# Layer 1: gate columns of all sixteen tiles first, the shared expert's up products afterwards from turned halves kept on chip

## The chip, the core and the metric

The kernel runs on one core of one Trainium2 chip. The metric is the device time of one execution, in microseconds (us); smaller is better. Engines are named as in the profile: PE (TensorE), PEld (its weight loads), DVE (VectorE), ACT (ScalarE), POOL (GpSimd) and SP (SyncE, which issues DMAs).

## What is computed

The input x has 4 x 512 tokens of 256 channels, here 16 tiles of 128 tokens. A mixture-of-experts block, a recurrent block and the same mixture-of-experts block again are added to it; the two passes through the first block are "layer 0" and "layer 1" below (`f` = 0 and 1).

```python
def ffn(x):                                   # x is layer-normalised
    scores = sigmoid(gate_w @ x) + gate_b     # 16 experts
    weights, indices = top_k(scores, 4); weights /= weights.sum(-1)
    shared = (silu(x @ w1_shared) * (x @ w3_shared)) @ w2_shared
    h3 = silu((x @ w1_routed[e]) * (x @ w3_routed[e]))     # for the 4 chosen e
    return shared + sum(weights * (h3 @ w2_routed[e]))
x = x + 0.5 * ffn(layernorm(x))
x = x + recurrence(layernorm(x))
x = x + 0.5 * ffn(layernorm(x))
```

## The kernel before

Everything is written out by hand: each engine has its own program, run in its order, and engines wait for each other by semaphores. The order of the code is the order of the work.

**The token phase of layer 1.** It runs from the end of the recurrence to the first expert tile. POOL normalises the 16 tiles (`norm`, L571). For each tile PE turns it into channels by tokens (`turn_x`, L1487, two transposes), ACT copies the result out of PSUM in a rounded format (the high half, `xs_high`, L741), and DVE subtracts to get the low half (`xs_low`, L1003). PE then forms the up products of the shared expert and the gate's logits in one accumulation of 2 x 176 + 16 = 368 columns (`hidden`, L1490, through `mm3`, L1414): three terms (high by high, low by high, high by low) for each of two channel halves, six matmuls, each with another 128-column stationary operand. The loop at L1582 turns tile s and then multiplies tile s - 2. ACT copies 16 logits (`logits`, L749) and applies silu to the first 176 columns (`silu`, L745), and DVE multiplies by the other 176, read from PSUM (`product`, L1008). SP writes the result to DRAM (`hid_out`, L471), where the end of the layer fetches it.

**The routing.** ACT applies the sigmoid to the logits of tiles 0 to 12 and of tiles 13 to 15 (`sigmoid`, L755). DVE takes the four best of 16 (`route_members`, L1033 to L1043), PE counts tokens per expert (`count`, L1558 and L1560), DVE works out each row's slot (`route_slots`, L1065 to L1099) and then, for each tile, builds two 0/1 matrices (`pick`, L1108 and L1110), which in layer 1 compare the table `hcst` with numbers in `stage`, both in SBUF. ACT scales one of them (`scale_pick`, L791), and PE multiplies them (L1574) into the list of token numbers, which DVE copies out at the end (L1121). Only then POOL begins to fetch rows by that list (`gather`, L578), and the loop over 79 expert tiles starts.

**The weights split again.** In layer 0 the weights of the routed experts are split into high and low parts. The recurrence overwrites those of experts 12 to 15. In layer 1 SP loads them again (`load_late`, L453 and L454), ACT makes the high parts (`high_expert`, L668 and L671), and POOL the low parts (`low_expert`, L547, 512 and 704 columns for an expert). PE waits for them before the first expert tile (L1606).

Of the kernel before, what the change touches and what calls it, by code (L numbers as in the profile page):

```python
# [7 lines left out]
H = 176  # L8
# [23 lines left out]
LAG_HID = 5  # L32
# [39 lines left out]
MW = 3 * DC * D  # L72
UP_AGAIN = [sum(e >= MAMBA_E for e in u) for u in (DVE_UP, POOL_UP)]
# [13 lines left out]
def build(nc, x_d, w13r_d, w2r_d, w13s_d, w2s_d, wm_d, cst_d, hcst_d, out_d):  # L87
# [7 lines left out]
    with ctx:  # L95
# [20 lines left out]
        mroom = nc.alloc_sbuf_tensor_at("mamba_room", [P, (NE - MAMBA_E) * 2 * WE], f32, offset=w_base + MAMBA_E * 2 * WE * 4)  # L116
        stage = [sb("stage0", [P, WSH]), sb("stage1", [P, WE])]
# [11 lines left out]
        hT = [[ring_r[:, 1024 + (b * 2 + h) * 256:1024 + (b * 2 + h + 1) * 256] for h in range(2)] for b in range(2)]  # L129
        ring_g = sb("ring_g", [P, (XG - UN) * D])  # L130
        xg = [ring_f[:, k * D:(k + 1) * D] for k in range(UN)] + [ring_g[:, k * D:(k + 1) * D] for k in range(XG - UN)]
# [79 lines left out]
        late = [w_routed[:, g, 0, :].bitcast(f32) for g in range(MAMBA_E, NE)]  # L211
        xn = [[late[(t // 4 + 2 * f) % 4][:, t % 4 * D:(t % 4 + 1) * D] for t in range(NT)] for f in range(2)]
# [14 lines left out]
        p_xA, p_hA = pb[0:2] + pb[6:8], pb[2:6]  # L227
        p_slot = pb[1][:, 0:256]
# [50 lines left out]
        s_a = sem("hidden_first")  # L279
        s_m = sem("hidden_product")  # L280
# [37 lines left out]
        def highs(f, e):  # L318

            return e - NHD + 1 if f == 0 else NE - NHD + e - MAMBA_E + 1  # L320
# [114 lines left out]
        def _(sp):  # L435
# [53 lines left out]
            for f in range(2):  # L489
                if f == 1:  # L490
                    sp.wait_ge(m_s["res"], NMC)
                for t in range(NT):
                    xn_out(f, t)
                    if f == 1 and t >= LAG_HID:
                        hid_out(f, t - LAG_HID)
                    if f == 0 and t in LATE_AFTER:
                        load_late(MAMBA_E + LATE_AFTER.index(t))
                for e in range(MAMBA_E if f else NE, NE):
                    load_late(e)
                for t in range(NT - LAG_HID if f else NT, NT):  # L500
                    hid_out(f, t)
# [43 lines left out]
        def _(pool):  # L545
# [27 lines left out]

            def gather(f, j):
# [80 lines left out]
        def _(act):  # L655
# [81 lines left out]
            def xs_high(f, t):  # L737
                act.wait_ge(s_xt, f * STEPS + t + 1)
                if t >= 4:
                    act.wait_ge(s_h, f * STEPS + t - 3)  # L740
                act.activation(xT4[t % 4][0], p_xA[t % 4][:, 0:DC * P], ACT.Copy).then_inc(s_xhi, 1)  # L741
# [9 lines left out]
            def sigmoid(f, n):  # L751

                first, end = ROUTED[n]
                act.wait_ge(s_lg, f * NT + end)
                act.activation(p_sig[n], rawlg[:, first * NE:end * NE], ACT.Sigmoid).then_inc(s_sig, 1)  # L755
# [39 lines left out]
            for f in range(2):  # L795
                base = f * STEPS
                for t in range(NT):
# [9 lines left out]
                    if f == 1 and t == 2:  # L807
                        next_root(1)
                        table(SET_SILU)
                    if t >= 3:  # L810
                        logits(f, t - 3)
                    if 3 <= t < LAST_SILU + 3:
                        silu(f, t - 3)
                    if t == LAST_SILU + 2:
# [5 lines left out]
                for t in range(NT - 3, NT):  # L820
# [6 lines left out]
                for t in range(LAST_SILU, NT):  # L827
# [5 lines left out]
                for e in range(MAMBA_E, NE if f else MAMBA_E):  # L833
                    high_expert(f, e)
# [108 lines left out]
        def _(dve):  # L943
# [57 lines left out]
            def xs_low(f, t):  # L1001
                dve.wait_ge(s_xhi, f * STEPS + t + 1)
                dve.tensor_tensor(xT4[t % 4][1], p_xA[t % 4][:, 0:DC * P], xT4[t % 4][0].bitcast(f32), ALU.subtract  # L1003
                                  ).then_inc(s_xlo, 1)
# [22 lines left out]
            def route_members(f):  # L1027
# [18 lines left out]
                for t in range(LAST_SILU, NT):  # L1046
# [71 lines left out]
            def route_end(f):  # L1118
# [4 lines left out]
                if f == 0:  # L1123
                    dve.wait_ge(s_et, NT)
                for b in range(4):
# [134 lines left out]
            for f in range(2):  # L1260
# [8 lines left out]
                for t in range(NT):  # L1269
# [11 lines left out]
                    if t >= 4:  # L1281
# [126 lines left out]
        def _(pe):  # L1408
# [80 lines left out]

            def hidden(f, t):  # L1490
                pe.wait_ge(s_xlo, f * STEPS + t + 1)
                if t >= 4:
                    pe.wait_ge(s_m, f * STEPS + t - 3)
                    pe.wait_ge(s_lg, f * NT + t - 3)
                b = t % 4
                mm3(p_hA[b][:, 0:GS], [(xT4[b][0][:, q * P:(q + 1) * P], xT4[b][1][:, q * P:(q + 1) * P],
                                        w_shared[:, 0, q * GS:(q + 1) * GS], w_shared[:, 1, q * GS:(q + 1) * GS])
                                       for q in range(DC)]).then_inc(s_h, 1)
# [218 lines left out]
```

## Time and profile before

| | us |
|---|---|
| median of 3 runs | 560.35 |
| lowest and highest | 560.19, 562.23 |
| the profiled execution's own time | 561.91 |
| its span, first to last instruction | 560.1 |
| granted TensorE clock over the span | 0.922 |
| PE busy | 481.5 (86%) |
| DVE busy | 436.5 (78%) |
| ACT busy | 367.2 (66%) |
| POOL busy | 352.7 (63%) |

The profile is one execution. Its span and its own time differ by 1.8 us, which lie around the span. Busy times are those of the whole span; the change touches only the stretch from 305 to 360 us of it.

### The profile page before, as it was taken

To read this page: it belongs to the slowest core of one execution; us is meant where nothing else is said; L and a number is where in the kernel's file an instruction comes from. 1 tells how busy PE (TensorE), PEld (TensorE's weight loads), DVE (VectorE), ACT (ScalarE), POOL (GpSimd) and SP (SyncE) were. 2 spreads that over 40 slices of the span, in tenths; PEclk is the share of its full clock that TensorE was granted. 3 is DMA by queue.
4 is the path that set the end of the run, shared out by engine and by line. 5 is a ranking of instruction groups with operands and counts; after the bars stand their busy time and mean duration, and the time that the engine had idled before them with its cause. 6 is when DMAs were issued, how large, how long until landed. Compare 5 with 4: busy or idle time off the path is not lost.

```text
span 560.1 us, 13322 instructions
## 1 busy us (share of the span) xinstructions
PE 481.5 (86%) x3206; PEld 449.0 (80%) x3207; DVE 436.5 (78%) x1464; ACT 367.2 (66%) x1109; POOL 352.7 (63%) x364
## 2 busy tenths in 40 slices
PE   2969569999999999958996960599999999999865
PEld 2857449999999999947884950389999999999754
DVE  5889857777889888875998579656777888887836
ACT  2687836777777777767874571656777777777610
POOL 3699947546777777766411416276457777777774
PEclk9999678999999999979999885579999999999988
DMA  8992044666665566654100480036445555666666
GB/s 274 393 393 99 30 121 127 180 170 184 176 201 169 167 169 171 179 150 113 57 2 19 134 262 17 21 112 178 138 138 169 169 169 173 169 161 174 178 186 209
DMA packets 61150, 88.27 MB, mean 158 GB/s; under 512 B 9499, under 2 KB 46363, under 8 KB 61107
## 3 DMA queue, kind: packets, MB, share of 16 engines
q0 software_dynamic: 13728, 37.50, 26.3%
q1 hardware_dynamic: 47379, 50.29, 26.2%
q8 instruction: 15, 0.25, 0.2%
q14 instruction: 28, 0.23, 0.1%
HBM read 57.22 MB, written 30.54 MB: 157 GB/s over the span
## 4 chain that ended last, share of the span: by engine, by line
PE 60%; DVE 16%; issue 10%; DMA 5%; POOL 4%; ACT 4%; SPq 0%; POOLq 0%; ACTq 0%; DVEq 0%
PE bank L1414 29%; PE bank L1465 15%; PE bank L1435 6%; POOL mamba_room L616 3%; PE bank L1476 3%; PE bank L1475 3%; DMA ys_scratch<-ring_f 2%; DVE xres L1144 2%; PE bank L1487 1%; DMA raw_shared<-in_w13s 1%; PE bank L1633 1%; DMA ring_f<-xn_scratch,tokidx 1%; PE bank L1551 1%; DVE stage L1039 1%; DVE ring_f L1110 1%
## 5 line engine op out<-in xcount | busy, mean ns | idle before, releaser
L1465 PE MATMUL bank<-w_routed,ring_r 128*128 x790 | 120.8, 283 | 5.0 <-DVE ring_r L990 4.5
L1465 PEld LDWEIGHTS bank<-w_routed,ring_r 128*128 128x128 f32 x790 | 110.4, 189 | 7.4 <-issue 7.4
L578 POOL DMA_INDIRECT ring_f<-xn_scratch,tokidx x80 | 77.2, 965 | 58.3 <-DVE tokidx L1121 22.5
L695 ACT ACTIVATE ring_r<-bank 128x256 fp32r<-128x256 f32 x158 | 60.8, 385 | 68.9 <-PE bank L1476 66.8
L1414 PE MATMUL bank<-w_routed,ring_r 128*128 x480 | 100.6, 346 | 0.0
L578 POOL DMA_INDIRECT ring_g<-xn_scratch,tokidx x78 | 74.5, 955 | 35.4 <-PE bank L1435 20.2
L1414 PE MATMUL bank<-w_routed,ring_x 128*128 x468 | 94.6, 337 | 0.0
L1414 PEld LDWEIGHTS bank<-w_routed,ring_r 128*128 128x128 f32 x480 | 78.8, 196 | 0.1
L1414 PEld LDWEIGHTS bank<-w_routed,ring_x 128*128 128x128 f32 x468 | 74.1, 190 | 0.0
L988 DVE TENSOR_TENSOR ring_r<-bank,ring_r 128x128 fp32r<-128x128 f32 x158 | 45.8, 290 | 30.5 <-ACT ring_r L695 28.6
L547 POOL TENSOR_TENSOR w_routed<-raw_routed,w_routed 128x512 fp32r<-128x512 f32 (+1 forms) x38 | 55.3, 1494 | 19.7 <-ACT w_routed L671 19.6
L713 ACT ACTIVATE ring_f<-bank 128x256 f32<-128x256 f32 x152 | 58.4, 384 | 7.6 <-DMA ys_scratch<-ring_f 6.6
L592 POOL DMA_INDIRECT stage<-ys_scratch,si x48 | 46.5, 968 | 16.7 <-issue 10.4
L702 ACT ACTIVATE stage<-bank 128x176 f32<-128x176 f32 x158 | 50.2, 318 | 5.7 <-PE bank L1414 5.5
L990 DVE TENSOR_TENSOR ring_r<-bank,ring_r 64x128 fp32r<-64x128 f32 x158 | 46.5, 294 | 2.1
L1414 PE MATMUL bank<-w_shared,ring_r 128*128 128x368 f32 x192 | 42.5, 365 | 3.9 <-DVE ring_r L1003 3.9
L980 DVE TENSOR_TENSOR ring_r<-bank,ring_r 128x256 fp32r<-128x256 f32 x80 | 34.0, 424 | 12.2 <-ACT ring_r L686 9.8
L1435 PE MATMUL bank<-cst,ring_f 128*128 128x128 f32 x160 | 32.6, 287 | 8.7 <-DMA ring_f<-xn_scratch,tokidx 8.7
L1414 PEld LDWEIGHTS bank<-w_shared,ring_r 128*128 128x128 f32 x192 | 34.4, 206 | 5.5 <-issue 3.4
L616 POOL DMA_INDIRECT mamba_room<-ys_scratch,si x32 | 31.2, 974 | 11.6 <-issue 8.8
L592 POOL DMA_INDIRECT raw_shared<-ys_scratch,si x32 | 30.9, 964 | 10.1 <-issue 7.9
L571 POOL TENSOR_SCALAR w_routed<-xres,rstd,nmr 128x256 f32<-128x256 f32 x32 | 19.0, 619 | 28.6 <-DVE nmr L1236 14.5
(190 smaller groups left out, 1075.5 us busy)
## 6 DMA issues: line engine op xcount, KB each, us to landing
ys_scratch<-ring_f SPq DMA_DIRECT2D x152, 128.0 KB
raw_routed<-in_w13r SPq DMA_DIRECT2D x6, 704.0 KB, 12.2
xn_scratch<-w_routed SPq DMA_DIRECT2D x32, 128.0 KB, 4.0
raw_routed<-in_w2r SPq DMA_DIRECT2D x6, 512.0 KB, 12.7
raw_routed<-in_w13r SPq DMA_DIRECT2D x8, 352.0 KB, 6.4
xres<-in_x_in SPq DMA_DIRECT2D x4, 512.0 KB, 7.3
raw_routed<-in_w2r SPq DMA_DIRECT2D x8, 256.0 KB, 7.2
shared_scratch<-raw_ring SPq DMA_DIRECT2D x16, 128.0 KB, 1.7
```

The lines of the kernel that those rows point to most:

```text
L547: return pool.tensor_tensor(w_routed[0:rows, e, 1, cols], raw_routed[e // 2][0:rows, e % 2, 1, cols], w_routed[0:rows, e, 0, cols].bitcast ...
L578: pool.indirect_dma_start(xg[j % XG], None, xn_dram, bass.IndirectOffsetOnAxis(ap=tokidx[:, j:j + 1], axis=0)).then_inc(s_g[j % XG], 16)
L592: pool.indirect_dma_start(early_rows[n % ROWS], None, ys_dram[0:tiles_before(t) * P, :], bass.IndirectOffsetOnAxis(ap=si[:, n:n + 1], axis ...
L616: pool.indirect_dma_start(room[:, q, :], None, ys_dram[0:tiles_before(t) * P, :], bass.IndirectOffsetOnAxis(ap=si[:, n:n + 1], axis=0)).th ...
L695: act.activation(hT[b][0], p_hT[b][:, 0:2 * P], ACT.Copy).then_inc(s_hhi, 1)
L702: act.activation(up[b], p_h[b][:, H:2 * H], ACT.Copy).then_inc(s_a, 1)
L713: act.activation(yb[b] if last < 0 else y_last[last], p_y[b][:, 0:D], ACT.Copy).then_inc(s_yo, 1)
L988: dve.tensor_tensor(hT[b][1][:, 0:P], p_hT[b][:, 0:P], hT[b][0][:, 0:P].bitcast(f32), ALU.subtract)
L990: dve.tensor_tensor(rest, p_hT[b][64:P, P:2 * P], rest.bitcast(f32), ALU.subtract).then_inc(s_hlo, 1)
L1414: last = pe.matmul(out, a, b, start=(q == 0), stop=(q == len(terms) - 1))
L1435: last = pe.transpose(p_xT[b][:, q * P:(q + 1) * P], xg[k][:, q * P:(q + 1) * P], ident)
L1465: last = pe.matmul(p_y[b][:, 0:D], a, v, start=(q == 0), stop=(q == 4))
```

## The change

In layer 1 the product of 368 columns is divided. First, in the loop that turns the tiles, PE multiplies only the 16 gate columns of tile s - 1 (`gates`), into one bank for tiles 0 to 12 and one for tiles 13 to 15, from which ACT's sigmoid now reads directly, so the 16 copies of logits go. The turned halves of all 16 tiles stay in SBUF: tiles 0 to 7 in the rooms of experts 15 to 12 that wait for weights, tiles 8 to 15 in rings of the expert loop. Then PE forms the 352 up columns of tiles 0 to 7 (`hidden`, three banks in turn), the routing's `count`, and the up columns of tiles 8 to 15. ACT takes both halves of a product out of PSUM (`halves`: silu of one, a copy of the other), and POOL multiplies them (`multiply`) in place of DVE. The weights of experts 15, 14, 13 and 12 are loaded as their rooms come free, and split after tiles 7, 11 and 15 (`HIGH_AFTER`); the wait of DVE ahead of `pick` narrows to one group of writes.

```diff
+HELD = 2 * (NE - MAMBA_E)
+LATE_AGAIN = tuple(range(NE - 1, MAMBA_E - 1, -1))
+HIGH_AFTER = {HELD - 1: LATE_AGAIN[:1], HELD + 3: LATE_AGAIN[1:2], NT - 1: LATE_AGAIN[2:]}
...
+        p_lg = [pb[5][:, 0:ROUTED[0][1] * NE], pb[4][:, 0:(NT - ROUTED[1][0]) * NE]]
...
-                    if f == 1 and t >= LAG_HID:
-                        hid_out(f, t - LAG_HID)
...
-                for e in range(MAMBA_E if f else NE, NE):
+                for k, e in enumerate(LATE_AGAIN if f else ()):
+                    sp.wait_ge(s_h, STEPS + 2 * k + 2)
                     load_late(e)
-                for t in range(NT - LAG_HID if f else NT, NT):
+                    for t in range(max(0, 2 * k - 1), 2 * k + 1):
+                        hid_out(f, t)
+                for t in range(HELD - 1 if f else NT, NT):
                     hid_out(f, t)
...
+            def multiply(t):
+
+                pool.wait_ge(s_a, STEPS + t + 1)
+                pool.tensor_tensor(hidk[t], third[t], hidk[t], ALU.mult).then_inc(s_m, 1)
...
-                for e in range(0 if f == 0 else MAMBA_E, NE):
+                for e in range(NE if f == 0 else 0):
                     low_expert(f, e)
+                for t in range(NT if f else 0):
+                    multiply(t)
+                    for e in HIGH_AFTER.get(t, ()):
+                        low_expert(f, e)
+                if f == 1:
+                    pool.wait_ge(s_m, STEPS + NT)
                 pool.wait_ge(s_ti, f + 1)
...
+                    if f == 1:
+                        act.wait_ge(s_m, STEPS + HELD)
                 act.activation(w_routed[:, e, 0, 0:W13], raw_routed[e // 2][:, e % 2, 1, 0:W13], ACT.Copy)
...
+            def halves(t):
+
+                act.wait_ge(s_h, STEPS + t + 1)
+                if 4 <= t < HELD:
+                    act.wait_ge(s_m, STEPS + t - 3)
+                act.activation(hidk[t], p_hA[t % 3][:, 0:H], ACT.Silu)
+                act.activation(third[t], p_hA[t % 3][:, H:2 * H], ACT.Copy).then_inc(s_a, 1)
...
-                for e in range(MAMBA_E, NE if f else MAMBA_E):
-                    high_expert(f, e)
+                for t in range(NT if f else 0):
+                    halves(t)
+                    for e in HIGH_AFTER.get(t, ()):
+                        high_expert(f, e)
...
-                    for g in range(NG):
-                        dve.wait_ge(s_hw[g], group(0))
+                    dve.wait_ge(s_hw[1], group(0))
...
+                if f == 1:
+                    if t == 2:
+                        pe.wait_ge(s_sig, 2 * len(ROUTED))
+                    if t >= 3:
+                        pe.wait_ge(s_a, STEPS + t - 2)
+                    by_token(f, t, p_hA[t % 3][:, 0:2 * H], 0, 2 * H).then_inc(s_h, 1)
+                    return
...
+            def gates(t):
+
+                pe.wait_ge(s_xlo, STEPS + t + 1)
+                n = int(t >= ROUTED[1][0])
+                t0 = t - ROUTED[n][0]
+                by_token(1, t, p_lg[n][:, t0 * NE:(t0 + 1) * NE], 2 * H, NE).then_inc(s_gt, 1)
...
-                    if s >= 2:
+                    if f == 0 and s >= 2:
                         hidden(f, s - 2)
+                    if f == 1 and 1 <= s <= NT:
+                        gates(s - 1)
+                for t in range(HELD if f else 0):
+                    hidden(f, t)
...
                 count(f)
+                for t in range(HELD if f else NT, NT):
+                    hidden(f, t)
```

The order of the instructions at the two places that the prediction rests on. First PE in layer 1, before; `x6` are the six matmuls of one tile, L1487 the transposes, L1558 and L1560 the counts, L1567 and L1574 the end of the routing.

```order
L1487 MATMUL bank<-cst,w_routed 128x128 x2
L1414 MATMUL bank<-w_shared,ring_r 128x368 x6
L1487 MATMUL bank<-cst,w_routed 128x128 x2
L1414 MATMUL bank<-w_shared,ring_r 128x368 x18
L1558 MATMUL bank<-ring_f,hcst 128x256 x4
L1560 MATMUL bank<-ring_f,hcst 128x16x16 x4
L1567 MATMUL bank<-stage,hcst 1x80 x2
L1574 MATMUL bank<-ring_f 128x79 x8
```

And PE there with the change (L1534 are the transposes, L1623 and L1625 the counts).

```order
L1534 MATMUL bank<-cst,w_routed 128x128 x2
L1461 MATMUL bank<-w_shared,ring_x 128x16 x6
L1534 MATMUL bank<-cst,w_routed 128x128 x2
L1461 MATMUL bank<-w_shared,again_g 128x16 x12
L1461 MATMUL bank<-w_shared,again_late 128x352 x48
L1623 MATMUL bank<-ring_f,hcst 128x256 x4
L1625 MATMUL bank<-ring_f,hcst 128x16x16 x4
L1461 MATMUL bank<-w_shared,ring_r 128x352 x24
L1461 MATMUL bank<-w_shared,ring_x 128x352 x12
L1461 MATMUL bank<-w_shared,again_g 128x352 x12
L1632 MATMUL bank<-stage,hcst 1x80 x2
L1639 MATMUL bank<-ring_f 128x79 x8
```

Each tile keeps its six stationary operands in the first loop, with 16 moving columns in place of 368, and gets six more later: 48 matmuls of 352 columns stand ahead of the counts and 48 between them and the picks.

Second POOL in layer 1, before: normalisation, the low parts of four experts, the gathers.

```order
L571 TENSOR_SCALAR w_routed<-xres,rstd,nmr 128x256 x16
L547 TENSOR_TENSOR w_routed<-raw_routed_55,w_routed 128x512
L547 TENSOR_TENSOR w_routed<-raw_routed_55,w_routed 128x704
L547 TENSOR_TENSOR w_routed<-raw_routed_55,w_routed 128x512
L547 TENSOR_TENSOR w_routed<-raw_routed_55,w_routed 128x704
L547 TENSOR_TENSOR w_routed<-raw_routed_56,w_routed 128x512
L547 TENSOR_TENSOR w_routed<-raw_routed_56,w_routed 128x704
L547 TENSOR_TENSOR w_routed<-raw_routed_56,w_routed 128x512
L547 TENSOR_TENSOR w_routed<-raw_routed_56,w_routed 128x704
L578 DMA ring_f<-xn_scratch,tokidx 128x256 x4
```

And POOL there with the change (L566 are the low parts, L596 the products of the shared expert).

```order
L590 TENSOR_SCALAR w_routed<-xres,rstd,nmr 128x256 x16
L596 TENSOR_TENSOR stage<-w_routed,stage 128x176 x8
L566 TENSOR_TENSOR w_routed<-raw_routed_56,w_routed 128x512
L566 TENSOR_TENSOR w_routed<-raw_routed_56,w_routed 128x704
L596 TENSOR_TENSOR raw_shared<-raw_ring,raw_shared 128x176 x2
L596 TENSOR_TENSOR hid_room<-raw_ring,hid_room 128x176 x2
L566 TENSOR_TENSOR w_routed<-raw_routed_56,w_routed 128x512
L566 TENSOR_TENSOR w_routed<-raw_routed_56,w_routed 128x704
L596 TENSOR_TENSOR hid_room<-raw_x,hid_room 128x176 x2
L596 TENSOR_TENSOR ring_f<-ring_g,ring_f 128x176 x2
L566 TENSOR_TENSOR w_routed<-raw_routed_55,w_routed 128x512
L566 TENSOR_TENSOR w_routed<-raw_routed_55,w_routed 128x704
L566 TENSOR_TENSOR w_routed<-raw_routed_55,w_routed 128x512
L566 TENSOR_TENSOR w_routed<-raw_routed_55,w_routed 128x704
```

The eight operations on weights now come after products that need tiles 7, 11 and 15, and so after `count`.

## Rows read from the trace of the kernel before

**Rows 1.** The chain that ended last, layer 1's start: start us, length us, what.

```profile
307.91 2.07 PE bank L1414 x6
309.97 0.43 PE bank L1487 x2
310.40 1.84 PE bank L1414 x6
...
314.89 0.22 PE bank L1487 x2
315.11 1.00 PE bank L1414 x6
...
334.20 1.03 PE bank L1558 x4
...
336.97 0.70 DVE ring_f L1065
...
349.72 0.32 DVE ring_f L1108
...
359.89 0.25 DVE tokidx L1121
...
368.61 1.76 PE bank L1414 x6
...
370.73 0.97 PE bank L1414 x6
```

**Rows 2.** Windows: length, busy us of PE, PEld, DVE, ACT, POOL; granted clock, DMA.

```profile
309.10:312.50 3.40, 3.40 (x14) 3.23 (x14) 2.08 (x5) 1.52 (x4) 3.40 (x7) 0.50 0.26 82
312.50:328.90 16.40, 16.40 (x106) 15.88 (x106) 8.89 (x33) 9.73 (x39) 1.67 (x4) 1.00 0.51 162
349.70:359.90 10.20, 6.85 (x64) 4.32 (x64) 9.20 (x33) 9.13 (x16) 0.00 (x0) 0.50 0.01 2
```

**Rows 3.** Timeline, PE and what follows it: start, us, engine, line, operation.

```profile
307.77 2.21 PE L1414 MATMUL bank<-w_shared,ring_r 128*128 128x368 f32 x6
309.77 0.63 PE L1487 MATMUL bank<-cst,w_routed 128*128 128x128 f32 x2
...
313.50 0.38 PE L1487 MATMUL bank<-cst,w_routed 128*128 128x128 f32 x2
...
314.34 0.42 DVE L1003 TENSOR_TENSOR ring_r<-bank,ring_r 128x256 fp32r<-128x256 f32 x1 [0.56 <-ACT ring_r L741]
...
350.78 0.27 PEld L1574 LDWEIGHTS bank<-ring_f 128*128 128x128 f16 x4 [1.81 <-DVE ring_f L1110]
```

**Rows 4.** Groups by line and form, ACT and POOL, 313 to 345 us: busy us, mean ns.

```profile
L745 ACT ACTIVATE stage<-bank 128x176 f32<-128x176 f32 x7 | 2.3, 324 | 0.0
L668 ACT ACTIVATE w_routed<-raw_routed 128x704 fp32r<-128x704 f32 x4 | 3.2, 796 | 0.7 <-DMA raw_routed<-in_w2r 0.7
L671 ACT ACTIVATE w_routed<-raw_routed 128x512 fp32r<-128x512 f32 x4 | 2.5, 622 | 0.0
L547 POOL TENSOR_TENSOR w_routed<-raw_routed,w_routed 128x704 fp32r<-128x704 f32 x4 | 6.7, 1672 | 0.0
L547 POOL TENSOR_TENSOR w_routed<-raw_routed,w_routed 128x512 fp32r<-128x512 f32 x4 | 5.1, 1263 | 19.2 <-ACT w_routed L671 19.2
```

**Rows 5.** Timeline, DVE beside POOL, in layer 0 and at the start of layer 1.

```profile
23.06 0.41 DVE L1014 CAST w_routed<-raw_routed 128x512 fp32r<-128x512 f32 x1
...
24.86 2.98 POOL L547 TENSOR_TENSOR w_routed<-raw_routed,w_routed 128x512 fp32r<-128x512 f32 x2
25.19 1.50 DVE L1014 CAST w_routed<-raw_routed 128x512 fp32r<-128x512 f32 x1
...
308.22 3.26 POOL L571 TENSOR_SCALAR w_routed<-xres,rstd,nmr 128x256 f32<-128x256 f32 x6
...
308.89 0.47 DVE L1230 TENSOR_TENSOR lg<-lg 128x2 f32<-128x2 f32 x1
```

More of the change, by code:

```diff
@@ L211, in build @@
         late = [w_routed[:, g, 0, :].bitcast(f32) for g in range(MAMBA_E, NE)]
+        kept = [(2 * (LATE_AGAIN[t // 2] - MAMBA_E) + 1) * WE + t % 2 * 512 for t in range(HELD)]
+        kept = [again_late[:, k:k + 512] for k in kept]
+        kept += [ring_r[:, b * 512:(b + 1) * 512] for b in range(4)]
+        kept += [ring_x[:, b * 512:(b + 1) * 512] for b in range(2)] + [again_g[:, b * 512:(b + 1) * 512] for b in range(2)]
+        kept = [(k[:, 0:256], k[:, 256:512]) for k in kept]
+        third = [late[t % 4][:, 1024:1024 + H] for t in range(HELD)]
+        third += [room[:, b * 512 + 256:b * 512 + 256 + H] for room, n in ((raw_ring, 4), (raw_x, 2), (ring_g, 2)) for b in range(n)]
         xn = [[late[(t // 4 + 2 * f) % 4][:, t % 4 * D:(t % 4 + 1) * D] for t in range(NT)] for f in range(2)]
@@ L318, in highs, with split @@
         def highs(f, e):
-            return e - NHD + 1 if f == 0 else NE - NHD + e - MAMBA_E + 1
+            return e - NHD + 1 if f == 0 else NE - NHD + LATE_AGAIN.index(e) + 1
+        def split(f, t):
+            return kept[t] if f else xT4[t % 4]
         def combined_before(f, t):
@@ L738, in xs_high @@
                 act.wait_ge(s_xt, f * STEPS + t + 1)
-                if t >= 4:
+                if f == 0 and t >= 4:
                     act.wait_ge(s_h, f * STEPS + t - 3)
-                act.activation(xT4[t % 4][0], p_xA[t % 4][:, 0:DC * P], ACT.Copy).then_inc(s_xhi, 1)
+                act.activation(split(f, t)[0], p_xA[t % 4][:, 0:DC * P], ACT.Copy).then_inc(s_xhi, 1)
             def silu(f, t):
@@ L753, in sigmoid @@
                 first, end = ROUTED[n]
-                act.wait_ge(s_lg, f * NT + end)
-                act.activation(p_sig[n], rawlg[:, first * NE:end * NE], ACT.Sigmoid).then_inc(s_sig, 1)
+                if f == 0:
+                    act.wait_ge(s_lg, end)
+                else:
+                    act.wait_ge(s_gt, end)
+                act.activation(p_sig[n], p_lg[n] if f else rawlg[:, first * NE:end * NE], ACT.Sigmoid).then_inc(s_sig, 1)
             def copy_early(n):
@@ L819, in _ @@
                 sigmoid(f, 0)
-                for t in range(NT - 3, NT):
+                for t in range(NT - 3 if f == 0 else NT, NT):
                     logits(f, t)
@@ L826, in _ @@
                 table(SET_SILU)
-                for t in range(LAST_SILU, NT):
+                for t in range(LAST_SILU if f == 0 else NT, NT):
                     silu(f, t)
@@ L1045, in route_members @@
                                   ie.unsqueeze(1).broadcast_to((P, NT * TOPK, NE)), ALU.is_equal).then_inc(s_mem, 1)
-                for t in range(LAST_SILU, NT):
+                for t in range(LAST_SILU if f == 0 else NT, NT):
                     product(f, t)
@@ L1124, in route_end @@
                     dve.wait_ge(s_et, NT)
+                else:
+                    for g in range(NG):
+                        dve.wait_ge(s_hw[g], group(0))
                 for b in range(4):
@@ L1280, in _ @@
                         scales(2, 8, NT)
-                    if t >= 4:
+                    if f == 0 and t >= 4:
                         product(f, t - 4)
@@ L1488, in turn_x, with by_token @@
                 last.then_inc(s_xt, 1)
-            def hidden(f, t):
-                pe.wait_ge(s_xlo, f * STEPS + t + 1)
-                if t >= 4:
[L1493 to L1498, printed above, removed]
+            def by_token(f, t, out, first, m):
+                hi, lo = split(f, t)
+                return mm3(out, [(hi[:, q * P:(q + 1) * P], lo[:, q * P:(q + 1) * P],
+                                  w_shared[:, 0, q * GS + first:q * GS + first + m], w_shared[:, 1, q * GS + first:q * GS + first + m])
+                                 for q in range(DC)])
+            def hidden(f, t):
+                if f == 1:
[5 more added lines that the diff above has]
+                    return
+                pe.wait_ge(s_xlo, t + 1)
+                if t >= 4:
+                    pe.wait_ge(s_m, t - 3)
+                    pe.wait_ge(s_lg, t - 3)
+                by_token(f, t, p_hA[t % 4][:, 0:GS], 0, GS).then_inc(s_h, 1)
+            def gates(t):
[3 more added lines that the diff above has]
+                by_token(1, t, p_lg[n][:, t0 * NE:(t0 + 1) * NE], 2 * H, NE).then_inc(s_gt, 1)
             def turn_early(n):
```

17 lines of the change are left out of this document (10 added, 7 removed).

## The prediction

> **What bounds the kernel now.** I read three views for the stretch from 305 to 360 us: the chain that ended last, the windows with their granted clock, and the timelines of the engines. The chain [rows 1] is one line of work with no slack. PE turns and multiplies tile after tile; DVE picks the four best experts; PE counts from 334.20; DVE computes slots from 336.97 to 349.72 and picks from there until the token list is copied out at 359.89. Only then can the first gather start. So whatever moves the first slot instruction (336.97), or stretches the picks, moves the end of the kernel by as much. The second thing to see is the clock [rows 2]. PE begins the phase at 1.2 GHz: it was granted 0.50 up to 312.5 us, though it was fully busy from 309, and 1.00 from then on. In the picks, where PE is busy 67% of the time with short matmuls, it has 0.50 throughout. The third is that POOL is idle in the picks [rows 2]: its low parts are done by then, and this hides a conflict, named below.
>
> **Step 1, the gate pass (PE).** At half clock a tile costs 0.43 us for its two transposes and 1.84 for six matmuls of 368 columns; at full clock 0.22 and 1.00 [rows 1]. The change keeps the transposes and the six stationary operands and cuts only the columns, from 368 to 16. What is left of each matmul is the load of its 128x128 operand, and the trace has no such matmul, so I bound it at half clock. Below: four f16 loads take 0.27 us together, 0.067 each [rows 3]. Above: a transpose, which also has a load of its own and 128 columns, takes 0.43 / 2 = 0.21 [rows 1]. Between them is the one load that nothing covers: the first six products, begun at 307.77, are followed by transposes at 309.77 [rows 3], which is 2.00 against 1.84 with the load covered, so 0.16. I take 0.16, since it is the same operand type. A tile is then 0.43 + 6 x 0.16 = 1.39; one load of six can run under the transposes, so about 1.3 us. By the lower price the turn-around binds instead: transposes begun at 313.50 end in a low half at 314.34 + 0.42 [rows 3], 1.26 us, to which tile t's transposes, its gates and those of a neighbour are tied two by two, which gives some 1.1 us a tile. By the upper price a tile is 1.7.
>
> Which clock? I take half. The phase begins at half as before, and PE then streams, per tile, two transposes and 6 x 16 columns: the rest is loading. The nearest stretch is the picks, where also many loads stand beside few columns, and it stayed at 0.50 for 10 us [rows 2]. The opposite is a rival.
>
> So the gates begin at 307.77, as the first product did, and need 16 x 1.3 = 20.8 us, plus about 0.5 for a table load of ACT after tile 2 that long products hid: they end near 329. The up products of the kernel before ended there too: a tile at full clock cost 1.00 + 0.22 = 1.22 us [rows 1]. The pass saves nothing because it loads as much as before.
>
> The Trainium skill (TensorE: Matmul & The Clock Gate, LDWEIGHTS) prices a load by its columns, 128 / 1.2 GHz = 107 ns at half clock. No run here shows it for this operand. By it, as an estimate, a tile would take the 1.1 us of the turn-around, the gates would end 3 us sooner, and the forecast would be 565.
>
> **Step 2, eight up products ahead of the count (PE).** Six matmuls of 352 columns take 1.76 us at half clock and 0.97 at full [rows 1]. Before, the clock rose 4.7 us after the first dense product (307.77 to 312.5). I take three tiles at 1.76 and five at 0.97: 10.1 us, so PE reaches the count near 339.2. DVE's picking of the best four begins when the gates are in, takes 6 us as before, and is done near 335. It must wait: this is new.
>
> **Step 3, the count.** It runs at full clock now, behind dense products: half of 336.97 - 334.20 = 2.77 us [rows 1], 1.4. The first slot instruction starts at 340.6 instead of 336.97: **+3.6 us**. By the bounds of a load it is +0.4 or +10.
>
> **Step 4, slots.** Its instructions are the same, 12.75 us to the first pick. PE's last eight products, 8 x 0.97 = 7.8 us, end inside it and cost nothing; if they ran at half clock (14 us) the picks would wait 1 to 2 us. The four products that DVE no longer makes lay beside the count and save nothing, nor do the 16 copies of logits, off the chain.
>
> **Step 5, POOL's queue.** A product of 176 columns is not in the trace on POOL; from 1.263 us for 512 and 1.672 for 704 [rows 4], 2.1 ns a column, I get 0.55. POOL now works in the order: products 0 to 7, weights of expert 15, products 8 to 11, expert 14, products 12 to 15, experts 13 and 12. Its first weights wait for PE's eighth product at 339.2, ACT's two copies (2 x 0.32), a product (0.55) and ACT's high part (0.80 + 0.62) [rows 4]: 342.0. From there 4 x 2.93 + 8 x 0.55 = 16.1 us follow without a gap, since ACT has its parts ready: POOL is done near 358. The picks begin at 340.6 + 12.75 = 353.35. So the last 4 to 5 us of POOL's weights lie beside the picks, where POOL was idle before.
>
> What that costs is shown elsewhere [rows 5]. A DVE cast of 512 columns within SBUF takes 0.41 us. The same cast, issued after POOL had begun a low part at 24.86, takes 1.50: it ends only after POOL's instruction does. A DVE instruction of two columns, both inputs in SBUF, takes 0.47 beside POOL's normalisation. Both instructions of a pick have two inputs in SBUF. I take it that each waits for the POOL instruction under way: three of these (0.3 to 1.7 us long) stand in the way, **+4 us** of the 4.7 that overlap. Below: nothing; above: all 4.7.
>
> The Trainium skill (SBUF — State Buffer, Who interferes with whom) states this as a rule: a VectorE instruction with two SBUF inputs and a GpSimd instruction that reads SBUF exclude each other, for the whole instruction. The casts above agree, 1.50 against 0.41; that f16 picks do the same no row shows.
>
> **Other edits.** SP loads experts 15 to 12 after two, four, six and eight up products, each some 3 us ahead of ACT's need or more: nothing. The writes of the shared expert's hidden rows leave later, but are fetched only after the first expert tiles: nothing. DVE's wait for one group of writes in place of four: nothing, since those rows are written by then.
>
> **The sum.** 3.6 + 4.0 = 7.6 us. The profiled execution took 561.91 (span 560.1), so 569.5 by its own time; it lay 1.56 above the median. Against the median of 560.35: **568.0 us**.
>
> **The rivals.**
>
> *The clock rises in the gate pass.* If loads of operands keep PE at 2.4 GHz, a tile is limited by the turn-around, 0.95 us; the gates end at 323, eight products (7.8) at 330.8, the count at 332.2: 4.8 us sooner than before, +4 in the picks: 559.6, not slower. It decides if the clock is 1.00 within the first six tiles. For it: PE is loading without a pause. Against it: the half clock of the picks, and the start at half clock.
>
> *The picks are not disturbed.* POOL ends before them (it would have to gain 4.7 us), or DVE's f16 instructions slip through between: 560.35 + 3.6 = 564. For it: in layer 0 POOL's low parts run beside the picks without harm, but there one input is in PSUM. Against it: the two casts.
>
> *Both rivals together*: 4.8 us sooner and nothing lost in the picks, 555.6, faster. *Loads at the upper price*: 6 us more in the gate pass, 574.
>
> **How the numbers follow.** Half clock and disturbed picks (the forecast): 0.56, of which 0.05 near 574. Half clock, picks undisturbed: 0.15, at 564, two thirds of them over the line. The clock rival with disturbed picks: 0.12, at 559.6. Both rivals: 0.07, at 555.6. The rest, 0.10, is a gate pass at the lower price or a clock that rises half-way, around 561. A measurement can tell 0.5%, 2.8 us, from no change: 557.5 to 563.2 counts as the same. Slower: 0.56 + 0.10 + 0.04 = 0.70. Same: 0.12 + 0.05 + 0.03 = 0.20. Faster: 0.10. The range leaves out the fastest rival and the upper price: 558 to 572.5. Within the forecast alone it is 564.5 to 572.5.
>
> **What would show it.** In the windows of the changed kernel: a granted clock of 0.50 from 306 to about 330, then 1.00 until the last up products (step 1). On the chain: transposes and six gate products at about 1.3 us a tile. DVE idle some 5 us between its best-four work and the first slot instruction, released by the count on PE (steps 2 and 3). PE busy through the slots. On DVE: picks of over 1 us, three or more, while POOL works on weights, and a pick stage of 14 us in place of 10.2 (step 5). The prediction is wrong if the clock is 1.00 by the sixth tile, if gates take under 1.1 us a tile, or if POOL is idle by the first pick.

## The result and the profile after

The changed kernel takes 573.1 us (median of 4 runs), the kernel before 560.3 beside it: a ratio of 1.024, with a 95% interval from 1.020 to 1.027, or 12.8 us more. Slower was forecast, but 568.0 was 5 us too low, and 573.1 lies just above the range's end of 572.5. The profiled execution of the changed kernel took 572.98 us, with a span of 571.1.

The chain that ended last, changed kernel, against [rows 1] (start us, length us, what):

```profile
312.60 0.34 DVE again_late L1049
312.98 1.45 PE bank L1461 x6
314.43 0.54 PE bank L1534 x2
314.97 1.08 PE bank L1461 x6
...
330.63 0.54 PE bank L1534 x2
331.17 11.53 PE bank L1461 x60
342.71 0.45 PE bank L1623 x4
343.16 0.88 PE bank L1625 x4
344.06 0.70 DVE ring_f L1110
...
356.65 4.47 POOL w_routed L566 x3
361.12 11.02 issue
372.14 0.99 POOL ring_f L602
```

L1534 are the transposes, L1461 the products, L1623 and L1625 the count, L1110 the first slot instruction. Three things are new. A tile of the gate pass costs 0.54 + 1.08 = 1.62 us. The slots begin at 344.06 in place of 336.97, 7.1 us later. And a POOL line, three low parts, stands on the chain where the picks stood. The 11.02 us of "issue" behind it are POOL's wait for the token list, for which this profile names no releaser, so the picks themselves do not appear.

The windows of the same kernel, against [rows 2] (busy us of PE, PEld, DVE, ACT, POOL, then granted clock and DMA):

```profile
305.70:336.40 30.70, 29.86 (x138) 28.81 (x139) 13.26 (x70) 9.95 (x24) 8.23 (x16) 0.50 0.21 69
336.40:344.00 7.60, 7.60 (x48) 7.19 (x48) 2.71 (x12) 3.68 (x14) 4.25 (x8) 1.00 0.79 237
356.90:371.20 14.30, 6.87 (x64) 4.34 (x64) 13.31 (x33) 9.12 (x16) 4.22 (x3) 0.50 0.00 1
```

The whole gate pass ran at 1.2 GHz, though PE was busy 97% of it. The clock rose only at 336.4, three microseconds into the up products. Before, it rose at 312.5.

Its timeline, DVE and POOL at the two turning points (in brackets the idle time before and what ended it):

```profile
344.06 0.69 DVE L1110 TENSOR_TENSOR_SCAN ring_f<-stage,bank 128x256 f32<-128x256 f32 x1 [4.64 <-PE bank L1625]
...
355.39 5.73 POOL L566 TENSOR_TENSOR w_routed<-raw_routed,w_routed 128x512 fp32r<-128x512 f32 x4
...
356.91 4.39 DVE L1153 TENSOR_TENSOR ring_f<-hcst,stage 128x316 f16<-128x316 f16 x1
361.23 0.41 DVE L1155 TENSOR_TENSOR ring_f<-hcst,stage 128x512 f16<-128x512 f16 x1
...
371.14 0.24 DVE L1166 CAST tokidx<-bank 128x79 int32<-128x79 f32 x1 [0.97 <-PE bank L1639]
```

DVE stands idle 4.64 us for the count. The first pick instruction, 0.32 us before, takes 4.39: it ends when POOL's four low parts end. The picks, from the first one's start to the list, take 14.2 us against 10.2.

The phase is compared by times from its first turn, layer 1's first transposes (306.14 before, 305.68 now), since executions differ by a microsecond in what lies ahead. The first slot instruction comes at 30.8 before and 38.4 now, the list at 53.7 and 65.5. Of these 11.7 us, 7.5 arise ahead of the slots, 0.1 in them and 4.1 in the picks. The first gather adds 0.5: it starts 1.0 us after the list's copy starts, 0.5 before. That makes 12.2. The rest of the 12.8 lies between executions: the profiled one before was 1.6 us above its median, while in the changed kernel's the phase began 0.5 earlier and what follows the first gather took 0.7 less.

### The profile page after: what moved, and what is told of

It is laid out like the page before. It is cut to its first block, busy times and chain, and to the rows that moved or that the text cites. A ratio compares the mean times of both kernels' runs of the same rounds, so it can differ in the third digit from the quotient of the medians.

```text
span 571.1 us, 13499 instructions
## 1 busy us (share of the span) xinstructions
PE 501.1 (88%) x3302; PEld 469.9 (82%) x3303; DVE 437.3 (77%) x1448; ACT 367.9 (64%) x1108; POOL 359.6 (63%) x380
## 4 chain that ended last, share of the span: by engine, by line
PE 65%; DVE 13%; issue 10%; DMA 4%; POOL 4%; ACT 3%; SPq 0%; POOLq 0%; ACTq 0%; DVEq 0%
PE bank L1461 31%; PE bank L1512 15%; PE bank L1482 6%; PE bank L1522 3%; PE bank L1523 3%; PE bank L1616 3%; POOL mamba_room L640 2%; PE bank L1534 2%; DVE xres L1192 1%; DMA ys_scratch<-ring_f 1%; PE bank L1704 1%; DMA ring_f<-xn_scratch,tokidx 1%; DMA raw_shared<-in_w13s 1%; POOL w_routed L566 1%; DVE ring_f L1160 1%
## 5 line engine op out<-in xcount | busy, mean ns | idle before, releaser
L727 ACT ACTIVATE ring_r<-bank 128x256 fp32r<-128x256 f32 x158 | 60.8, 385 | 67.4 <-PE bank L1523 67.1
L1461 PE MATMUL bank<-w_routed,ring_r 128*128 x480 | 100.0, 345 | 0.0
L1461 PE MATMUL bank<-w_routed,ring_x 128*128 x468 | 94.6, 337 | 0.0
L1461 PEld LDWEIGHTS bank<-w_routed,ring_r 128*128 128x128 f32 x480 | 78.5, 195 | 0.0
L1461 PEld LDWEIGHTS bank<-w_routed,ring_x 128*128 128x128 f32 x468 | 74.0, 190 | 0.0
L566 POOL TENSOR_TENSOR w_routed<-raw_routed,w_routed 128x512 fp32r<-128x512 f32 (+1 forms) x38 | 55.5, 1491 | 2.1 <-ACT w_routed L703 2.0
L1025 DVE TENSOR_TENSOR ring_r<-bank,ring_r 128x256 fp32r<-128x256 f32 x80 | 33.9, 424 | 12.6 <-ACT ring_r L718 10.2
L616 POOL DMA_INDIRECT raw_shared<-ys_scratch,si x32 | 30.7, 959 | 10.1 <-issue 7.9
L590 POOL TENSOR_SCALAR w_routed<-xres,rstd,nmr 128x256 f32<-128x256 f32 x32 | 18.9, 607 | 28.6 <-DVE nmr L1284 14.5
L718 ACT ACTIVATE ring_r<-bank 128x256 fp32r<-128x256 f32 x80 | 30.5, 381 | 9.9 <-PE bank L1482 9.8
L1025 DVE TENSOR_TENSOR ring_x<-bank,ring_x 128x256 fp32r<-128x256 f32 x78 | 33.1, 424 | 4.3 <-ACT ring_x L718 1.8
## 6 DMA issues: line engine op xcount, KB each, us to landing
raw_routed<-in_w13r SPq DMA_DIRECT2D x6, 704.0 KB, 12.3
raw_routed<-in_w2r SPq DMA_DIRECT2D x6, 512.0 KB, 12.8
```

Source lines behind the costliest of these rows:

```text
L566: return pool.tensor_tensor(w_routed[0:rows, e, 1, cols], raw_routed[e // 2][0:rows, e % 2, 1, cols], w_routed[0:rows, e, 0, cols].bitcast ...
L616: pool.indirect_dma_start(early_rows[n % ROWS], None, ys_dram[0:tiles_before(t) * P, :], bass.IndirectOffsetOnAxis(ap=si[:, n:n + 1], axis ...
L727: act.activation(hT[b][0], p_hT[b][:, 0:2 * P], ACT.Copy).then_inc(s_hhi, 1)
L1025: dve.tensor_tensor(xT[b][1], p_xT[c % 2][:, 0:DC * P], xT[b][0].bitcast(f32), ALU.subtract).then_inc(s_xlo, 1)
L1461: last = pe.matmul(out, a, b, start=(q == 0), stop=(q == len(terms) - 1))
```

## The experiments

Theory 1: the gate pass is dear because it loads as many operands as before, at half clock. Theory 2: the picks wait for POOL's low parts. All kernels start from the changed one or the one before, as each says; ratios are to the kernel before, run on the same chip (the changed kernel: 1.024).

**Three gate products in place of six.** From the changed kernel.

```diff
+                if m > NE:
+                    return mm3(out, pairs)
+                terms = [(pairs[0][0], pairs[0][2]), (pairs[0][1], pairs[0][2]), (pairs[1][0], pairs[1][2])]
```

> Leaves out three of the six products of each tile's gate columns, so the logits are rougher; nothing else is changed. Theory 1 (the gate pass is paced by TensorE's weight loads at half clock): the changed kernel took 1.62 us per tile for eight loads (two of transposes, six of gates), so three loads fewer are worth 3 x 0.18 to 3 x 0.216 = 0.54 to 0.65 us per tile, pace 0.97 to 1.08 us, granted clock still 0.50 through the pass. Over the 13 steady tiles the first slot instruction comes 7.0 to 8.4 us earlier (344.1 to about 336), the total is 573.1 to about 565.5 us. Price of 0.16 per load, as I had predicted: 6.2 us. Rival (the turn through ScalarE and VectorE, 0.38 + 0.42 us and their handovers, paces the pass): pace stays near 1.6 us, total stays at 573.

Measured: 568.2 us, ratio 1.011 [1.009, 1.013], some 7 us less than the changed kernel by ratio; first slot instruction 6.7 us earlier from the first turn. The clock was 0.50 until 329.8. Its chain:

```profile
315.74 0.54 PE bank L1534 x2
316.28 0.44 PE bank L1547 x3
316.72 0.54 PE bank L1534 x2
317.26 0.76 PE bank L1547 x3
```

One tile takes 0.98 us, the next 1.30. The first is what loads predict: (1.62 - 0.98) / 3 = 0.213 us for each load taken away. In the second, PE waits 0.32 us for the low half: the turn through ACT and DVE, the rival, comes next, close behind. So with six products the pass is paced by its loads, 0.213 us for each product of 16 columns.

**GpSimd relieved.** From the changed kernel: POOL multiplies one column instead of 176 for tiles 8 to 15.

```diff
+                m = H if t < HELD else 1
+                pool.tensor_tensor(hidk[t][:, 0:m], third[t][:, 0:m], hidk[t][:, 0:m], ALU.mult).then_inc(s_m, 1)
```

> GpSimd multiplies one column in place of 176 for tiles 8 to 15, so the shared hidden of these tiles is left unfinished; 8 x 0.56 us go from GpSimd, 0.3 or so stays. Theory 2 (the first pick instruction on VectorE waits 4.39 us because GpSimd still runs the low parts of two experts until 361.1): GpSimd ends about 357.2, the first pick instruction takes under 1 us, the list of tokens is complete 3.5 to 4.0 us earlier, total 569.3. Rival (the first pick waits for ScalarE, a transfer or a semaphore): still about 4.4 us, total 573.

Measured: ratio 1.018 [1.013, 1.023], which touches that of the changed kernel, so the time alone settles nothing. In the trace the picks take 12.3 us, 2.0 less than in the changed kernel. POOL ended 53.7 us after the first turn, 1.7 sooner than in the changed kernel and not the expected 3.9: its low parts now wait 0.78 and 0.34 us for ACT's high parts, which I had not counted. So only half of the gain came.

**The count after four up products.** From the changed kernel.

```diff
-                for t in range(HELD if f else 0):
+                for t in range(AHEAD if f else 0):
                     hidden(f, t)
```

> TensorE makes four up products ahead of the count in place of eight; the other four come behind it. The first slot instruction comes about 4 us earlier (344.1 to about 340), VectorE's idle 4.6 us ahead of it goes. Theory 2: the last low part on GpSimd hangs on the up products, which the count now delays by 1.4 us, so GpSimd ends at about 362.5 and the first pick waits about 9 us for it: total 573.1 + 1 = 574 us, no gain. Rival (the place of the count sets the end): total 569.

Measured: 576.0 us, ratio 1.025 [1.022, 1.027]. The first slot instruction came 3.9 us earlier (34.5 from the first turn), the list at the same 65.5. What was won ahead of the slots was lost in the picks, as theory 2 said. DVE and POOL in its timeline:

```profile
353.44 1.78 DVE L1154 TENSOR_TENSOR ring_f<-hcst,stage 128x316 f16<-128x316 f16 x1
...
357.59 6.28 POOL L567 TENSOR_TENSOR w_routed<-raw_routed,w_routed 128x512 fp32r<-128x512 f32 x4
357.73 1.49 DVE L1156 TENSOR_TENSOR ring_f<-hcst,stage 128x512 f16<-128x512 f16 x1
359.14 1.79 DVE L1154 TENSOR_TENSOR ring_f<-hcst,stage 128x316 f16<-128x316 f16 x1
...
363.97 0.41 DVE L1156 TENSOR_TENSOR ring_f<-hcst,stage 128x512 f16<-128x512 f16 x1
```

Here the two engines take turns, a pick for each low part, and not in the one long wait that was expected, until POOL is done at 363.9; then a pick takes 0.41 again.

**Low parts earlier, products last.** From the changed kernel.

```diff
-HIGH_AFTER = {HELD - 1: LATE_AGAIN[:1], HELD + 3: LATE_AGAIN[1:2], NT - 1: LATE_AGAIN[2:]}
+HIGH_AFTER = {HELD - 1: LATE_AGAIN[:1], HELD: LATE_AGAIN[1:2], HELD + 2: LATE_AGAIN[2:3], HELD + 4: LATE_AGAIN[3:]}
```

> The low parts of the last three experts on GpSimd (and their high parts on ScalarE) follow tiles 8, 10 and 12 in place of 11, 15 and 15; the work is the same, but what GpSimd does beside the first picks is products of 0.56 us in place of low parts of 1.45 us. Theory 2, blocked as long as GpSimd has anything to run: first pick waits until about 361, total 573. Rival, GpSimd and VectorE take turns by instruction: the picks go on from 357 with a wait of about 0.5 us each, the list is complete 2 to 3 us earlier, total 570 to 571.

Measured: ratio 1.022 [1.020, 1.024], no difference from the changed kernel that can be told. The engines do take turns, and still only 0.7 us comes of it in the trace (list at 64.8). This other order of POOL's work made little difference; less of it, with GpSimd relieved, gave 2.0.

**The conflict alone.** From the kernel before: one wait holds POOL's last two experts back until the slots are known.

```diff
+                    if f == 1 and e == NE - 2:
+                        pool.wait_ge(s_te, 2)
                     low_expert(f, e)
```

> The kernel before, with one wait added: GpSimd makes the low parts of the last two experts only after VectorE has the slots, that is beside the picks; nothing of the gate pass is in it. Theory 2: their four instructions take 5.73 us, from about 348.9 us, of which 4.9 us lie behind the first pick's start at 349.7; the list is complete 4.5 to 4.9 us later and the total is 4.7 us longer (ratio 1.008). Rival (picks and low parts run side by side, or the longer picks of the changed kernel came from elsewhere): ratio 1.000, the list at the same time.

Measured: ratio 1.010 [1.006, 1.013], 5.4 us (3.5 to 7.2 by the interval). Its timeline:

```profile
349.02 0.62 DVE L1110 TENSOR_TENSOR ring_f<-hcst,stage 128x316 f16<-128x316 f16 x1
349.57 1.89 DVE L1112 TENSOR_TENSOR ring_f<-hcst,stage 128x512 f16<-128x512 f16 x1
...
348.20 6.09 POOL L547 TENSOR_TENSOR w_routed<-raw_routed,w_routed 128x512 fp32r<-128x512 f32 x4 [9.75 <-DVE si L1096]
```

The picks take 14.5 us, 4.3 more; the list is 3.2 us later from the first turn, since in this execution the clock rose 2.3 us sooner after that turn and the first slot instruction came 1.1 sooner. With nothing of the gate pass in it, this prices step 5 by itself. Over the runs, in us (the time from the start of the picks to POOL's end, and how much longer than 10.16 the picks take; the runs not listed are like the changed kernel where 4.2 us are left, and like the kernel before where nothing is):

| run | POOL left | picks longer |
|---|---|---|
| before | 0 | 0 |
| last eight tiles (below) | 1.1 | 1.0 |
| relieved | 2.5 | 2.1 |
| changed kernel | 4.2 | 4.1 |
| low parts earlier | 4.7 | 3.5 |
| conflict alone | 5.3 | 4.3 |
| count after four | 10.4 | 8.0 |

**Gate columns first for the last four tiles.** From the kernel before: tiles 0 to 11 as they were; gates of 12 to 15, then their up products, then the count. The first routing group is 12 tiles.

```diff
+                if f == 1 and t >= FIRST:
+                    by_token(f, t, p_gate(f, t), 2 * H, NE).then_inc(s_gt, 1)
+                    return
...
+                for t in range(FIRST, FIRST + AHEAD if f else 0):
+                    up_late(t)
```

> The kernel before, with the gate columns made first for the last four tiles alone (their up products follow behind the last gate columns, ahead of the count, from the same ring of turned halves); the first group for routing is 12 tiles in place of 13. Theory 1 says that what a gate pass costs hangs on the clock in which it runs. At full clock a tile takes about 0.27 + 6 x 0.107 = 0.91 us (half of the 0.213 of the slow clock) in place of 1.23, the last routing group starts 1.2 us sooner: first slot instruction 1.2 us earlier, ratio 0.998. If the clock drops in these four tiles, they take 1.62 us each and the up products behind them 1.76: slower by 1.5 us or more, ratio 1.003.

Measured: ratio 1.000 [0.998, 1.002]. The first slot instruction came 0.95 us sooner, though the clock fell for 3.4 us at 329.0, just behind the four narrow tiles, the last of which had come after a gap of 1.11 us on PE. A microsecond lies at the edge of what these runs can tell.

**Gate columns first for the last eight tiles.** The same with `FIRST = 8`; four up products stand ahead of the count, four behind it, whose halves POOL multiplies.

> As the run with the last four tiles, but with the gate columns first for the last eight: four up products ahead of the count, four behind it (these multiplied on GpSimd, from halves that ScalarE copies); the experts are loaded and split as in the kernel before, so that GpSimd is done before the picks. At full clock throughout: eight tiles at 0.91 in place of 1.23 us, first slot instruction 2.2 us earlier, ratio 0.996. If the clock drops behind the first few narrow tiles, the rest take 1.62 us: first slot instruction 0 to 3 us later, ratio 1.000 to 1.006.

Measured: ratio 1.000 [0.999, 1.002]. The first slot instruction came 0.7 us sooner, and the picks took 1.0 longer beside what POOL had left. Its windows, and two tiles of the gate pass at full clock on PE's timeline:

```profile
309.20:318.30 9.10, 9.10 (x62) 8.89 (x60) 5.78 (x17) 5.35 (x22) 4.89 (x10) 0.99 0.35 111
318.30:323.10 4.80, 4.18 (x40) 3.97 (x38) 2.15 (x7) 3.33 (x11) 0.00 (x0) 1.00 0.57 184
323.10:333.30 10.20, 10.20 (x42) 10.20 (x43) 7.31 (x56) 3.63 (x13) 0.00 (x0) 0.50 0.85 290
...
319.16 0.81 PE L1461 MATMUL bank<-w_shared,ring_r 128*128 128x16 f32 x6
319.83 0.44 PE L1534 MATMUL bank<-cst,w_routed 128*128 128x128 f32 x2
320.02 0.81 PE L1461 MATMUL bank<-w_shared,ring_r 128*128 128x16 f32 x6
```

At full clock a gate tile takes 0.86 us (319.16 to 320.02), and a load (319.83 - 319.16) / 6 = 0.112. Then the clock fell in the fifth narrow tile and stayed down for 10 us, into the up products. PE had one gap of 0.62 us ahead of that, in the fourth tile. So the narrow products do not merely begin at half clock; here it fell while they ran. Whether the gap had a part in it, this run alone does not tell.

**The changed kernel with 256 columns per gate product.** 240 up columns are multiplied along and thrown away; the tiles write to four banks in turn, from which ACT copies the 16 logits as in the kernel before (that part of the edit is left out here).

```diff
-                by_token(1, t, p_lg[n][:, t0 * NE:(t0 + 1) * NE], 2 * H, NE).then_inc(s_gt, 1)
+                by_token(1, t, p_hA[t % 4][:, 0:WIDE], GS - WIDE, WIDE).then_inc(s_gt, 1)
```

> The changed kernel, whose gate products now run over 256 columns (240 up columns ahead of the 16 gate columns, thrown away) into a bank of their own per tile, from which ScalarE copies the 16 logits as in the kernel before. At half clock 256 columns take 0.213 us, as much as the load that they stand beside, so nothing gets slower; at full clock 0.107 beside a load of 0.111. Theory 1 in its second half (the pass is dear because TensorE's clock stays at 0.50 while it makes 16 columns per load, and comes back with wide products): the granted clock is 1.00 from about 312 us as in the kernel before, a tile takes 0.9 to 1.0 us in place of 1.62, the first slot instruction comes at 334 to 336 in place of 344.1, total 573.1 - 9 = 564 us, ratio 1.004 to 1.009 to the kernel before (the wait at the picks stays). Rival (the clock has other reasons, or falls with loads): clock 0.50 as before through the pass, ratio 1.024.

Measured: 567.4 us, ratio 1.010 [1.007, 1.012], a little above the 1.004 to 1.009 that was expected. Windows and chain:

```profile
307.30:314.10 6.80, 6.38 (x28) 5.66 (x28) 3.48 (x9) 3.19 (x8) 6.80 (x13) 0.50 0.65 215
314.10:328.50 14.40, 13.75 (x102) 11.95 (x100) 6.69 (x25) 6.15 (x28) 1.22 (x3) 1.00 0.14 45
...
317.72 0.22 PE bank L1536 x2
317.94 0.72 PE bank L1463 x6
318.66 0.22 PE bank L1536 x2
318.87 0.97 PE bank L1463 x6
```

With sixteen times the columns the pass is faster: 1.07 us a tile (2.13 for two) in place of 1.62, at a clock of 1.00 from 314.1. The first slot instruction comes at 30.6 us from the first turn, 7.8 sooner and level with the kernel before. By the span's own time it is 337.9, later than the 334 to 336 expected; 1.6 us of that is the later start of the phase in this execution, the rest a pace above 0.9 to 1.0. Banks and copies changed here with the columns; the next run has the columns alone. What is left is the picks, 14.2 us as in the changed kernel.

**The last eight tiles, with 256 columns.** From the run with the last eight tiles; only the columns, and with them their place in the bank, differ.

```diff
-                    by_token(f, t, p_gate(f, t), 2 * H, NE).then_inc(s_gt, 1)
+                    c = 0 if t >= 12 else GS - WIDE
+                    by_token(f, t, p_hA[t % 4][:, c:c + WIDE], GS - WIDE, WIDE).then_inc(s_gt, 1)
```

> The run with the gate columns first for the last eight tiles, its gate products widened to 256 columns in the same way. There the clock fell to 0.50 at 323.1 us, in the sixth of the eight narrow tiles, and came back at 333.3. Theory 1: it stays at 1.00 into the count, the last three tiles take 0.86 in place of 1.28 us and the four up products behind them 0.97 in place of 1.76, the first slot instruction comes 2 to 3 us earlier than in the kernel before, ratio 0.995. Rival: the clock falls all the same, ratio 1.000.

Measured: 557.5 us, ratio 0.9925 [0.990, 0.995]: 4.2 us faster than the kernel before, and it beats both.

```profile
318.30:325.70 7.40, 6.98 (x60) 6.77 (x60) 3.95 (x20) 4.73 (x17) 0.00 (x0) 1.00 0.60 185
325.70:330.00 4.30, 4.00 (x26) 3.71 (x24) 4.09 (x42) 2.80 (x8) 0.00 (x0) 1.00 0.93 303
...
332.86 0.68 DVE L1113 TENSOR_TENSOR_SCAN ring_f<-stage,bank 128x256 f32<-128x256 f32 x1
```

The clock holds at 1.00 through the gate pass, the up products and the count, with a gap of 0.42 us on PE at the place where the run with narrow products had 0.62 (the clock fell there in the fifth narrow tile by its rows, not in the sixth, as the expectation has it). A longer gap, 1.05 us ahead of the count at 330.75, left the clock at 1.00 here as well. A wide tile takes 0.93 us, a narrow one at the same clock 0.86: the columns are nearly free, not quite. The first slot instruction comes at 27.0 us from the first turn, 3.8 before the old place; POOL is done before the picks, which take 10.2 us.

**Both causes taken from the changed kernel.** From the 256-column run: the low parts of the last two experts are left out, ACT writes zeros.

```diff
+                if f == 1 and e in LATE_AGAIN[2:]:
+                    return
...
+                                act.activation(w_routed[:, e, 1, cols], raw_routed[e // 2][:, e % 2, 1, cols], ACT.Copy,
+                                               scale=0.0).then_inc(s_wlo, 1)
```

> The run with the 256 column gate products in the changed kernel, with the low parts of the last two experts left out: ScalarE writes zeros for them ahead of the picks (some 2.8 us, until about 351), GpSimd does nothing beside the picks. If the clock and the low parts beside the picks are the whole loss, the list of tokens is complete about 54 us after the layer's first turn, as in the kernel before (53.75; 57.7 with the low parts), and the ratio falls from 1.0095 to 1.000 to 1.003. If something else of the change still costs (the eight up products ahead of the count, the reload of the experts), it stays above 1.005.

Measured: ratio 1.0005 [0.998, 1.003].

```profile
335.27 0.69 DVE L1118 TENSOR_TENSOR_SCAN ring_f<-stage,bank 128x256 f32<-128x256 f32 x1 [3.10 <-PE bank L1633]
348.16 0.33 DVE L1161 TENSOR_TENSOR ring_f<-hcst,stage 128x316 f16<-128x316 f16 x1
...
358.32 0.24 DVE L1174 CAST tokidx<-bank 128x79 int32<-128x79 f32 x1 [0.97 <-PE bank L1647]
```

The first turn was at 304.63: the list is complete 53.7 us later, as before, and the picks take 10.2. So the two causes are the whole loss, as far as the interval can tell; the 0.5 us ahead of the first gather are still there (359.31, 1.0 after the list's copy starts).

## Why the prediction was right and wrong

**Step 1, the gate pass: the mechanism was right, the price was not.** The pass is bound by loads at half clock, as said. But the step took 0.16 us for a load, and it is 0.213: 0.54 + 1.08 = 1.62 us a tile, not 1.3. With 0.213 the step's own sum gives 1.5 to 1.7. The pass, from the first gate product at 307.31 to the first up product at 333.40, took 26.1 us where 21.3 was said (20.8 and 0.5 for the table load, behind which PE paused 0.44). This term alone is 4.8 us; 0.5 was hidden by the phase's earlier start in this execution, and the up products gave 0.9 back. So the first slot instruction accounts for 3.5 of the 5 us by which the forecast was low, slots and picks for 0.2 and the gather for 0.5. The rest is the distance between executions named above: 1.6 in the median that was started from, less the 0.7 behind the first gather. What was nearest is the rival that the prediction called the upper price, 574 us.

```profile
329.20 1.43 PE L1461 MATMUL bank<-w_shared,ring_x 128*128 128x16 f32 x6
330.49 0.69 PE L1534 MATMUL bank<-cst,w_routed 128*128 128x128 f32 x2
...
333.40 9.30 PE L1461 MATMUL bank<-w_shared,again_late 128*128 128x352 f32 x48
```

Six loads from 329.20 to 330.49 make 0.215 each. The bound that I had worked out from above, half a pair of transposes, 0.21, was the right row, for it is the same kind of load beside a short matmul. I chose the middle row instead, 2.00 against 1.84, and gave the upper price a chance of 0.05. The middle row measured no load at all, for it took one number from the timeline and the other from the chain. The timeline of the kernel before has the second tile's products, too:

```profile
310.05 2.19 PE L1414 MATMUL bank<-w_shared,ring_r 128*128 128x368 f32 x6
312.04 0.61 PE L1487 MATMUL bank<-cst,w_routed 128*128 128x128 f32 x2
```

From the start of the products to that of the next transposes are 1.99 us here and 2.00 for the first tile: no difference. In the chain alone [rows 1] it is 2.07 against 1.84, which would have given 0.23. That a load gets cheaper at full clock was taken for granted in the clock rival, without a price; it does, 0.112.

The Trainium skill (TensorE: Matmul & The Clock Gate, LDWEIGHTS) prices a load at P / 1.2, here 107 ns, and names no clock for it; I had read it as the price at half clock. The trace is near it at full clock, 0.112, and differs at half, 0.213, where the measurement decides.

**Which clock.** Half was right, for 30.7 us. The rival that loads alone would raise it fell: 0.50 well past the sixth tile. The run with 256 columns beside the same loads stood at 1.00 from 314.1.

**Steps 2 and 3.** The eight up products took 9.2 us, from 333.4 to 342.6, where 10.1 was said: the clock rose sooner. The count took 1.5 (342.55 to 344.06), as said (1.4), and DVE's idle time of 4.64 stands where 5 was said. The first slot instruction moved by 7.1 (7.5 from the first turn), not 3.6.

**Step 4.** The slots took 12.85 us to the first pick, against 12.75, so nothing was lost there.

**Step 5, the picks.** +4.0 was said and 4.1 measured. POOL had 4.2 us left at the first pick (4.7 said), the low parts' order and a product of 0.56 us (0.55 said) were right too. The form differs: not three picks of over 1 us, but a single one of 4.39, through three POOL instructions. So that 4.0 met 4.1 is in part luck: in other runs 4.7 and 5.3 us left cost 3.5 and 4.3. The rule of the Trainium skill (SBUF — State Buffer, Who interferes with whom), two SBUF inputs on VectorE against a GpSimd instruction that reads SBUF, holds for the f16 picks too: picks of 1.38 to 1.89 us beside a whole low part, 0.31 to 0.41 alone. The casts that the prediction held beside it have one input, so they showed the two engines excluding each other, but not for two inputs. Layer 0 of the kernel before shows the other side: there a pick of 512 columns has one input in PSUM, and it takes 0.68 us beside POOL's low parts (at 60.47) and after them (at 73.41) alike. Whether picks of layer 1 that read from PSUM would save the 4.1 us was not tried.

**Not foreseen.** 0.5 us between the list and the first gather. It shows in every run from the changed kernel and in none from the one before, also where POOL had nothing left beside the picks; its cause stays open.

## What to carry to other kernels

A matmul with few columns cost here what its operand's load costs (0.213 us at half clock, 0.112 at full), so splitting off narrow columns adds whole loads; price such a load by the nearest row where a load stands beside a short matmul, at the clock of that stretch, and not by a difference between two seams. Look at the granted clock of every stretch that gets narrower: here columns that nothing uses, nearly free beside the load, brought a pass from 1.62 to 1.07 us a tile. And add up what an engine with a shared resource still has queued when a critical stage begins: here seven to ten tenths of that remainder were lost, and the one other order that was tried changed little.

## What the runs showed of the hardware

- The granted clock fell with PE busy 4.18 of 4.80 us: 1.00 to 0.50 at 323.1 us in the run with eight narrow tiles, in 16-column products. The stretch of gate products with 256 columns (6.98 of 7.40 us busy) kept 1.00.
- Beside a queue of POOL low parts, DVE's picks were held in two ways: one instruction through three POOL instructions (4.39 us in the changed kernel, 4.35 and 4.38 in the runs with three gate products and with 256 columns), or in turns (1.38 to 1.89 us beside a whole low part, in four other runs). What decides between them was not tried. Both cost about the same in sum.
